# Attention heads' units in the order plain, plain, latent, latent, one 256-column product for the last plain block of two heads, and ACT's transposed copies ahead of a weight copy

## The reference

```
q = rope(x @ w_q)            # 32 heads of 128
k = rope(x @ w_k); v = x @ w_v       # 8 key heads, each shared by 4 query heads
lk = rope((x @ w_lq) @ w_lk); lv = x @ w_lv   # 32 "latent" key and value heads
attn = causal_attn(q, k, v)          # "plain"
lat  = causal_attn(q, lk, lv)        # "latent"
x = layernorm(x + attn @ w_o + lat @ w_lo)
```

## Time and profile before

| | us |
|---|---|
| median of 3 runs | 2455.63 (2455.56 to 2456.3) |
| the profiled execution | 2456.53 |
| its span, first to last instruction | 2454.7 |
| PE busy | 2441.0 (99%) |
| DVE busy | 1721.7 (70%) |
| ACT busy | 1116.3 (45%) |
| POOL busy | 894.8 (36%) |

### The profile page before, as it was taken

One profiled execution on the slowest core, in us unless ns is written; L12 is line 12 of the kernel. 1 busy time (PEld: TensorE's weight loads), 2 busy tenths in 40 slices (PEclk: granted clock), 3 DMA queues, 4 the chain that ended last, 5 costly groups with the idle time before them and its releaser, 6 DMA issues.

```text
span 2454.7 us, 40396 instructions
## 1 busy us (share of the span) xinstructions
PE 2441.0 (99%) x12295; PEld 2066.0 (84%) x12300; DVE 1721.7 (70%) x3599; ACT 1116.3 (45%) x2564; POOL 894.8 (36%) x676
## 2 busy tenths in 40 slices
PE   9999999999999999999999999999999999999999
PEld 7888888888888888888878888888888888888877
DVE  7767767677676767766787675776677676767666
ACT  4544445353444435344554444535444453544551
POOL 4343342424334242433533434253343425334210
PEclk9999999999999999999999999999999999999999
DMA  6222232313223231323423323232222323224411
GB/s 202 70 87 73 77 95 60 105 58 94 64 77 94 66 103 54 100 61 109 132 88 119 93 83 102 73 108 66 88 88 81 107 68 109 68 86 147 158 35 69
DMA packets 122823, 222.06 MB, mean 90 GB/s; under 512 B 12912, under 2 KB 21232, under 8 KB 122608
## 3 DMA queue, kind: packets, MB, share of 16 engines
q1 hardware_dynamic: 117536, 211.93, 28.6%
q10 hardware_dynamic: 5200, 9.18, 1.1%
HBM read 202.18 MB, written 18.87 MB: 90 GB/s over the span
## 4 chain that ended last, share of the span: by engine, by line
PE 95%; DVE 3%; issue 1%; ACT 0%; DMA 0%; SPq 0%; DVEq 0%; ACTq 0%
PE bank_a L1354 17%; PE bank_a L1356 16%; PE bank_a L1355 16%; PE bank_b L1355 13%; PE bank_b L1356 13%; PE bank_b L1354 13%; PE bank_b L1416 5%; PE bank_b L1743 1%; PE bank_a L1489 1%; PE bank_b L1678 0%; DMA w_raw<-wstream 0%; DVE q_lo L901 0%; DVE probs L894 0%; DVE probs L893 0%; PE bank_b L1726 0%
## 5 line engine op out<-in xcount | busy, mean ns | idle before, releaser
L477 POOL TENSOR_TENSOR w_lo<-w_raw,w_hi 128x512 fp32r<-128x512 f32 x612 | 815.3, 1340 | 1362.7 <-ACT w_hi L549 1341.0
L549 ACT ACTIVATE w_hi<-w_raw 128x512 fp32r<-128x512 f32 x616 | 383.7, 628 | 269.3 <-DMA w_raw<-wstream 139.2
L591 ACT ACTIVATE probs<-probs,row_min 128x512 f32<-128x512 f32 (+3 forms) x512 | 282.2, 553 | 474.0 <-DVE row_min L911 474.0
L1354 PE MATMUL bank_a<-w_hi,o_hi 128*128 128x512 f32 x1024 | 414.6, 405 | 1.4 <-DVE o_lo L933 1.4
L1356 PE MATMUL bank_a<-w_hi,o_lo 128*128 128x512 f32 x1024 | 402.0, 393 | 0.0
L1355 PE MATMUL bank_a<-w_lo,o_hi 128*128 128x512 f32 x1024 | 401.1, 392 | 0.0
L928 DVE TENSOR_TENSOR pT_lo<-bank_b,pT_hi 128x512 fp32r<-128x512 f32 (+1 forms) x384 | 207.2, 595 | 180.7 <-ACT pT_hi L597 180.7
L922 DVE TENSOR_SCALAR probs<-probs,row_inv 128x512 f32<-128x512 f32 (+3 forms) x512 | 256.5, 561 | 4.5
L1356 PEld LDWEIGHTS bank_a<-w_hi,o_lo 128*128 128x128 f32 x1024 | 192.3, 188 | 41.3
L911 DVE CUSTOM_DVE_ANT_0 probs<-bank_b,mask_sb 128x512 f32<-128x512 f32 (+3 forms) x512 | 221.5, 482 | 4.9 <-PE bank_b L1356 3.8
L1354 PEld LDWEIGHTS bank_a<-w_hi,o_hi 128*128 128x128 f32 x1024 | 193.4, 189 | 35.4 <-DVE o_lo L933 2.3
(11 more groups left out here) (196 smaller groups left out, 4758.0 us busy)
## 6 DMA issues: line engine op xcount, KB each, us to landing
w_raw<-wstream SPq DMA_DIRECT2D x615, 256.0 KB, 2.7
stage<-ctx SPq DMA_DIRECT2D x32, 256.0 KB, 2.7
stage_w<-wf SPq DMA_DIRECT2D x32, 256.0 KB, 2.8
q_scratch<-stage_q SPq DMA_DIRECT2D x32, 128.0 KB, 1.7
wf_hi_scratch<-piece_hi SPq DMA_DIRECT2D x16, 256.0 KB, 3.0
wf_lo_scratch<-stage_w SPq DMA_DIRECT2D x16, 256.0 KB, 3.3
wf_hi<-wf_hi_scratch SPq DMA_DIRECT2D x8, 512.0 KB, 7.6
wf_lo<-wf_lo_scratch SPq DMA_DIRECT2D x8, 512.0 KB, 8.6
```

What stands on the lines that cost most here:

```text
L477: nc.gpsimd.tensor_tensor(w_lo[:, s], w_raw[:, r], w_hi[:, s].bitcast(F32), ALU.subtract).then_inc(lo_done, 1)
L549: nc.scalar.activation(w_hi[:, s], w_raw[:, r], ACT.Copy).then_inc(hi_done, 1)
L591: nc.scalar.activation(part, part, ACT.Exp, bias=row_min[:, u % 2, i:i + 1], scale=-1.0, accum_out=row_sum[:, u % 2, i:i + 1]).then_inc(ex ...
L1354: nc.tensor.matmul(dst, still[0], move[0], start=start, stop=False)
```

## The change

In the 14 groups that are not first, the units come plain, plain, latent, latent: units 0 and 1 are the plain attention of heads 0 and 1, units 2 and 3 their latent one, and 4 to 7 the same for heads 2 and 3 (`unit`, and from it the order of the output weights in the DRAM stream). What follows from it:

- `scores`: both plain units of a pair of heads now make the 256-column product (plain and latent first block). The latent part is used only two units later, so DVE masks it right away into a buffer of its own, `first_scores`: five masks in a plain unit, three in a latent one.
- `transposes`: for the two plain units the last key block goes into bank b2 beside block 2, so that the pieces are 512, 384 and 384 columns; the 384-column pieces of the two units lie side by side in `last_hi` and `last_lo`, with both units' last block in the middle, 256 columns in a row.
- `values`: a plain unit makes only `kt` = 0 to 2. Unit 1 (and 5) first makes one product of 256 columns for `kt` = 3 of both heads, into bank b2 (`last_made`).
- The last 128 columns of a plain unit's output are thus a sum of two places. ACT parks those of the first head (`last_out`, 128 columns), `o_high` and `o_low` take 384 columns, DVE adds up (`last_sum`, two instructions, `last_sum_of_second`, one), ACT and DVE split the result (`last_high`, `last_low`, 256 columns, at unit 2 and 6).
- ACT: at even `c` in these groups `pT_high(u)` comes before `high_ahead` (`transposed`).
- New waits: PE's transposes of units 2 and 6 on `last_read`, values of 2 and 6 on `last_summed`, the first output part of each half on `last_lo_done`; DVE's last mask of units 3 and 7 on `last_made`. The first groups step these semaphores once at their end, on PE after a `drain`.

```diff
+LAST = 2000
+PT_A = [(0, 0, 0, 0, 512), (1, 1, 0, 512, 384), (2, 2, 0, LAST, 256), (3, 2, 256, LAST + 256, 128)]
+PT_B = [(0, 0, 0, 0, 512), (1, 1, 0, 512, 384), (3, 2, 0, LAST + 384, 128), (2, 2, 128, LAST + 512, 256)]
...
-    return (u % HG, u // HG) if first else (u // 2, u % 2)
+    return (u % HG, u // HG) if first else (2 * (u // 4) + u % 2, u % 4 // 2)
...
+def masked_before(G, u, first):
+    return 4 * UNITS * G + (4 * u if first else 16 * (u // 4) + (0, 5, 10, 13)[u % 4])
...
+def pT_pieces(u, first):
+    if first or u % 4 >= 2:
+        return PT_BANKS
+    return [(0, 0, 512), (1, 512, 384), (2, LAST + 384 * (u % 2), 384)]
...
+                    qt, _, at, w = TRI[i]
+                    part, low = probs[:, u % 2, at:at + w], row_min[:, u % 2, i:i + 1]
+                    of = part
+                    if latent and qt == 0:
+                        of, low = first_scores[:, u % 2], first_min[:, u % 2:u % 2 + 1]
+                    else:
+                        act.wait_ge(masked, before + (min(i, 2) if latent else i) + 1)
+                    nc.scalar.activation(part, of, ACT.Exp, bias=low, scale=-1.0,
...
-                    nc.scalar.activation(pT_hi[:, at:at + w], BANK_B[bank][:, 0:w], ACT.Copy).then_inc(pT_hi_done, 1)
-            def o_high(G, u):
+                    nc.scalar.activation(pT_part(at, w)[0], BANK_B[bank][:, 0:w], ACT.Copy).then_inc(pT_hi_done, 1)
...
+                w = N
+                if not first and u % 4 < 2:
+                    w = N - P
+                    if u % 2 == 0:
+                        nc.scalar.activation(last_out[:, 0], BANK_B[3][:, w:N], ACT.Copy)
+                nc.scalar.activation(o_hi[:, u, 0:w], BANK_B[3][:, 0:w], ACT.Copy).then_inc(o_hi_done, 1)
+            def last_high(G, j):
+                act.wait_ge(last_summed, 2 * G + j + 1)
+                nc.scalar.activation(o_hi[:, 4 * j:4 * j + 2, N - P:N], last_out[:], ACT.Copy).then_inc(last_hi_done, 1)
...
+                    transposed = not first and c > C_PREV + 1 and c % 2 == 0
+                    if transposed:
+                        pT_high(G, (c - C_PREV - 2) // 2, first)
                     high_ahead(b, g, c, tg)
...
+                            if not first and u % 4 == 2:
+                                last_high(G, u // 4)
...
-                    col = at - N * bank if qt else PAIR_AT + P * (u % 2)
-                    dve.wait_ge(scores_ready, scores_made(G, u, i))
+                    if qt == 0 and not first and u % 4 >= 2:
+                        continue
+                    col = at - N * bank
+                    if qt == 0:
+                        col = PAIR_AT + P * (u % 2) if first else PAIR_AT
...
+                    dve.wait_ge(scores_ready, scores_made(G, u, i, first))
+                    if not first and u % 4 == 3 and bank == 2:
...
                     dve.sem_inc(scores_seen, 1)
-                    nc.vector.tensor_tensor_reduce(
-                        out=probs[:, u % 2, at:at + w], in0=BANK_B[bank][:, col:col + w],
-                        in1=mask_sb[:, N - w:N], scale=-SCALE, scalar=3.4e38, op0=ALU.add, op1=ALU.min,
...
+                    block(first_scores[:, u % 2], BANK_B[2][:, PAIR_AT + P:PAIR_AT + 2 * P], P,
+                          first_min[:, u % 2:u % 2 + 1])
...
                 dve.wait_ge(o_hi_done, UNITS * G + u + 1)
-                nc.vector.tensor_tensor(o_lo[:, u], BANK_B[3][:], o_hi[:, u].bitcast(F32),
+                w = N if first or u % 4 >= 2 else N - P
+                nc.vector.tensor_tensor(o_lo[:, u, 0:w], BANK_B[3][:, 0:w], o_hi[:, u, 0:w].bitcast(F32),
...
+                made = BANK_B[2][:, PAIR_AT:PAIR_AT + 2 * P]
+                dve.wait_ge(o_hi_done, UNITS * G + 4 * j + 1)
+                nc.vector.tensor_tensor(last_out[:, 0], made[:, 0:P], last_out[:, 0], ALU.add)
+                nc.vector.tensor_copy(last_out[:, 1], made[:, P:2 * P]).then_inc(last_read, 1)
+            def last_sum_of_second(G, j):
+                dve.wait_ge(last_read, 2 * G + j + 1)
+                nc.vector.tensor_tensor(last_out[:, 1], BANK_B[3][:, N - P:N], last_out[:, 1],
+                                        ALU.add).then_inc(last_summed, 1)
+            def last_low(G, j):
+                dve.wait_ge(last_hi_done, 2 * G + j + 1)
+                nc.vector.tensor_tensor(o_lo[:, 4 * j:4 * j + 2, N - P:N], last_out[:],
+                                        o_hi[:, 4 * j:4 * j + 2, N - P:N].bitcast(F32),
+                                        ALU.subtract).then_inc(last_lo_done, 1)
...
                         normalise(G, u + 1)
+                    if not first and u % 4 == 2:
+                        last_low(G, u // 4)
                     if u in (0, 2) and not first:
                         add_part(b, p + u // 2, u // 2, chunk(b, g, C_PREV + 4 + 2 * u), False)
...
+                    if not first and u % 4 == 1:
+                        last_sum(G, u // 4)
                     if u + 1 < UNITS:
-                        o_low(G, u)
+                        o_low(G, u, first)
+                    if not first and u % 4 == 1:
+                        last_sum_of_second(G, u // 4)
...
-                    if u % 2 and qt == 0 and not first:
+                    if latent and qt == 0 and not first:
                         continue
...
+                    pe.wait_ge(last_read, 2 * G + u // 4 + 1)
+                places = pT_places(u, first)
+                for n, (kt, bank, col, _, _) in enumerate(places):
                     for qt in range(kt, TT):
-                        src, dst = row[qt] + P * kt, at - N * bank + P * (qt - kt)
+                        src, dst = row[qt] + P * kt, col + P * (qt - kt)
...
+                plain = not first and not latent
+                if not first and u % 4 == 2:
+                    pe.wait_ge(last_summed, 2 * G + u // 4 + 1)
+                if plain and u % 2:
+                    product(BANK_B[2][:, PAIR_AT:PAIR_AT + 2 * P], (v_hi[:, TT - 1], v_lo[:, TT - 1]),
+                            pT_part(LAST + 256, 256), True, True).then_inc(last_made, 1)
+                for kt, _, _, at, w in sorted(pT_places(u, first)):
                     if not latent:
...
+                    if plain and kt == TT - 1:
+                        continue
+                    last = product(BANK_B[3][:, P * kt:N], v, pT_part(at, w), kt == 0,
+                                   kt == TT - (2 if plain else 1))
...
                     if i == 0:
                         pe.wait_ge(o_lo_done, UNITS * G)
+                        pe.wait_ge(last_lo_done, 2 * G)
                     output(b, g, C_PREV + i, C_PREV + i, i, p, 4, queries_out)
...
+                    if i == 0 and not first:
+                        pe.wait_ge(last_lo_done, 2 * G + 1)
...
+                if first:
+                    nc.tensor.drain().then_inc(last_made, 2)
```

More of the change, by code:

```diff
@@ L584, in rotated_high, with exponentials @@
                 nc.scalar.activation(hi, rope_at(i, late), ACT.Copy).then_inc(rope_hi, 1)
-            def exponentials(G, u, blocks=(0, 1, 2, 3)):
+            def exponentials(G, u, first, blocks=(0, 1, 2, 3)):
+                before, latent = masked_before(G, u, first), not first and u % 4 >= 2
                 for i in blocks:
-                    _, _, at, w = TRI[i]
-                    act.wait_ge(masked, 4 * (UNITS * G + u) + i + 1)
-                    part = probs[:, u % 2, at:at + w]
-                    nc.scalar.activation(part, part, ACT.Exp, bias=row_min[:, u % 2, i:i + 1], scale=-1.0,
+                    qt, _, at, w = TRI[i]
[6 more added lines that the diff above has]
+                    nc.scalar.activation(part, of, ACT.Exp, bias=low, scale=-1.0,
@@ L707, in group @@
                 late = b == 0 and not tg
+                first = not tg
                 def latent_values_high():
@@ L756, in group @@
                         if c % 2 == 0:
-                            if not (late and u == 1):
-                                pT_high(G, u)
+                            if not transposed and not (late and u == 1):
+                                pT_high(G, u, first)
+                            if not first and u % 4 == 2:
+                                last_high(G, u // 4)
                         else:
                             if u + 2 < UNITS:
-                                exponentials(G, u + 2, (0, 1))
-                            o_high(G, u)
+                                exponentials(G, u + 2, first, (0, 1))
+                            o_high(G, u, first)
                             if u + 2 < UNITS:
-                                exponentials(G, u + 2, (2, 3))
+                                exponentials(G, u + 2, first, (2, 3))
                         if b and not tg:
@@ L768, in group @@
                         piece_high(2 * g + (12, 29).index(c))
-                pT_high(G, UNITS - 1)
+                pT_high(G, UNITS - 1, first)
+                if first:
```

(17 more changed lines are left out.)

88 lines of the change are left out of this document (59 added, 29 removed).

## The result

The changed kernel takes 2490.46 us (median of 4 runs, 2489.73 to 2491.25), the one before 2455.97 beside it: ratio 1.0139, with an interval of 1.0127 to 1.0151. Forecast were 2446.6 us, and the slower rival had 2462.0. The profiled execution has a span of 2488.6 us, at the full clock, as before.

A forecast was written before the change was run, and what follows sets the result against it. PE, 99% busy, was taken to bound the kernel. 9.0 us less for narrow matmuls, 0.3 less for late weight loads, 0.3 more for drains: 9.0 less than 2455.63, so 2446.6 us; range 2444.9 to 2451.2.

The forecast's parts named there:

- the slower rival: At both pairs, DVE's small steps and ACT's parked copy cost more, so PE waits 0.55 us: 2462.0 us; chance 5%.
- The narrow matmuls: On PE, two 128-column products of 0.34 us replaced by one 256-column of 0.36: 0.32 us a pair, 9.0 us less.
- The rival that a matmul costs by its columns: On PE, six 128-column matmuls are worth three of 256, so nothing is gained: 2455.6 us; chance 4%.
- The slack from unit 0 to unit 1: `pT_lo` ends 0.13 us before scores(3) with the moved copy; 0.4 us late with the old order on ACT.
- The weight copy that is now behind the transposed copies: ACT's weight copy starts about 1.8 us later, POOL and SP's load move with it; costed at nothing.
- The sign that the prediction named for this step: If the later weight copy were not free, POOL's low parts would show up among PE's waits.
- Its general sign: Wrong if PE's waits on `pT_lo`, the masks or `last_read` have grown to more than a few us.
- DVE has room at units 2 and 6: Added `last_low` and a mask at unit 2, 0.35 and 0.21 us, use 0.56 of 1.06 us slack.
- the 0.5 us of the masks in the stage of unit 0: DVE's masks of latent unit 2 end at 1541.17, leaving transposes(1), which wait for them, 0.5 us of slack.
- The drain: On PE at the end of the first groups: 0.16 us each, two of them 0.3 us more.
- The late weight loads: PE's late steps after scores(3), 0.07 us a group, 1.0 us in 14 groups; 0.3 us counted back.

The follow-up runs named there:

- The split product: The gated kernel with the 256-column product of a pair of heads made as two of 128 columns: 2455.43 us, ratio 0.9999.
- gated kernel: The changed kernel with both of ACT's weight copies of each unit made only after DVE has normalised that unit: 2446.34 us, ratio 0.9961; again 2446.18 us.

## Why the prediction was wrong, point by point

- *The narrow matmuls, 0.32 us a pair, 9.0 us*: right. The split product costs 9.1 us more, and the gated kernel is 9.4 (another time 10.4) us faster than before. The rival that a matmul costs by its columns is out.
- *The slack from unit 0 to unit 1*: right in its size. With the old order on ACT PE waits there (0.44 us, 0.4 forecast). In the gated kernel, where the copy is moved as well, PE's wait is gone; but there `normalise` is also shorter, and no run parts what the move pays from what the shorter `normalise` does.
- *"The weight copy that is now behind the transposed copies ... I cost it at nothing"*: this is the step that failed. It was priced by who waits for the copy: POOL, SP, PE, with 1362.7 us of idle time on POOL. None of them pays more than 0.9 us. What was not asked is which instructions of another engine the moved one then runs beside, and whether their durations hold. They don't: in each of 14 groups `normalise` goes from 1.94 to 2.98 us six times, and from 2.36 to 3.89 once. The sign that the prediction named for this step ("POOL's low parts would show up among PE's waits") would have missed it: they appear there once, with 0.9 us; DVE's results do. Its general sign, waits on `pT_lo` or the masks of more than a few us, did come.
- *DVE has room at units 2 and 6, 1.06 us of slack of which 0.56 is used*: the 0.5 us left is less than the 1.04 us that `normalise` grew by. The same holds for the 0.5 us of the masks in the stage of unit 0, where it grew by 1.5. So what stands behind `normalise` on DVE became late: the masks first of all, and in the stage of unit 0 the adds into `acc`.
- *The slower rival* had the right engine and the wrong cause (small steps dearer than their rows) and stopped at 2462.0. Between the changed kernel and the gated one, which has all of its instructions, lie 44 us.
- *The drain*, 0.16 us by the overlap of two matmuls: 0.75 us in place, mis-sized by a factor of five, in all at most 1.2 us.
- *The late weight loads, 0.3 us back of 1.0*: too little. A group of the gated kernel is 0.81 us shorter than before, where two pairs of heads at 0.325 us make 0.65. The other 0.16 us, some 2 us in 14 groups, is more than all that the prediction counted as late; no run shows how it is made up.

The number forecast, 2446.6 us, is what the kernel takes once the low parts keep off `normalise` (2446.34 and 2446.18). That it comes so near is partly luck, since the last two misses, of 1.2 and some 2 us, go against each other. The trace of before held the warning: `normalise` takes 1.94 us in most units and 1.27 in the first group, and its 512-column multiplication has a mean of 981 ns, for 541 in the gated kernel. An instruction that takes longer in one place than in another at the same shape may be held by something, and a sum that uses its duration has to say by what.

## What to carry to other kernels

Before moving an instruction off a critical path, ask not only who waits for it, but what it and its successors on other engines will run beside. When GpSimd and VectorE both work from SBUF, an idle GpSimd is not a free one. Put GpSimd's SBUF work beside VectorE's PSUM reads, with a semaphore if need be. If a change has two parts, time each alone: here the fusion was worth 9 us and the move spoilt it.

## What the runs showed of the hardware that was not expected

- A GpSimd low part (128 x 512, 1.29 us) holds a VectorE multiplication from SBUF to SBUF until it is done: one of 384 columns took 1.45 us, with a mean of 0.53 in the gated kernel. VectorE's steps that read PSUM kept their time beside it (`pT_lo` 1.62 us, an add into `acc` 0.68).
- Four GpSimd instructions of half the width hold four VectorE instructions, with 0.62 to 0.92 us for each.
- Six 128-column matmuls cost 0.325 us more than three of 256 columns, of the same data.
- A drain on PE between the transposes and a product that would else follow at once cost 0.75 us.
